# Weight preparation placed beside the first chunk's front, new step tables, and three element-wise steps moved from VectorE to GpSimd in a two-layer recurrent kernel

## What is computed

```python
x = L0_attn_x                                       # (2, 2048, 256)
xn = _layernorm(x)
s = _L0_attn_ref(xn, ...)                           # norm, Mamba block, norm, MLP 256-1024-256
g = _silu(_L0_ffn_ref(xn, w_gate, w_up, w_down))    # FP4-quantized gated MLP, 704 wide
x = x + s * g
xn = _layernorm(x)
s = _L1_attn_ref(xn, ...)                           # 16 heads, attention between the 2 sequences
g = _silu(_L1_ffn_ref(xn, qweights, scales, ...))   # 3 blocks of two 4-bit linears with LoRA
return x + s * g

def _mamba(x, ...):                                 # D_INNER 512, D_STATE 16, 4 taps
    xi, z = jnp.split(x @ in_proj_w, 2, axis=-1)
    xc = _silu(causal_conv(xi, conv_w) + conv_b)
    dt, Bm, Cm = jnp.split(xc @ x_proj_w, [16, 32], axis=-1)
    dt = jax.nn.softplus(dt @ dt_proj_w + dt_proj_b)
    h = exp(dt_t * A) * h + dt_t * B_t * x_t        # for each token t, 512 x 16 states
    y = sum(h * C_t) + D * xc
    return (y * _silu(z)) @ out_proj_w

def fp4_linear(x, w): return fp4(x) @ fp4(w).T      # blocks of 16: amax/6, round to E2M1, scale back
def _qlora_linear(x, q, scale, bias, la, lb):
    return x @ ((q / 7.5 - 1) * scale).T + bias + (x @ la.T) @ lb.T
```

## Time and profile before

| | |
|---|---|
| time, median of 3 runs | 1854.18 us (1853.78 to 1857.8) |
| profiled execution | 1856.52 us, of which the span of the profile is 1854.7 us |
| mean granted clock of PE over the span | 0.953 of full |
| busy share | PE 85%, DVE 84%, ACT 78%, POOL 68% |
| preparation of weights | 0 to 135.6 us |
| front of chunk 0 | 135.6 to 184.5 us |
| steady state | 99.65 us a chunk (861.65 to 961.30) |
| tail | 1757.0 to 1854.7 us |

### The profile page before, as it was taken

How to read it: one execution, slowest core, us unless ns; L and a number is a source line. 1 busy time by engine, 2 the same in 40 slices (tenths; PEclk the granted TensorE clock), 3 DMA queues, 4 the chain that set the end, 5 groups by cost and what they waited for, 6 DMA issues and landing times.

```text
span 1854.7 us, 28175 instructions
## 1 busy us (share of the span) xinstructions
PE 1577.4 (85%) x7632; PEld 1164.4 (63%) x7632; DVE 1551.4 (84%) x2882; ACT 1437.5 (78%) x3076; POOL 1252.4 (68%) x1313
## 2 busy tenths in 40 slices
PE   0083768899999999999989999999989999999875
PEld 0051556586767677776767676767667767767653
DVE  0623999999999999999999999999999999999811
ACT  0034678898989898989889888989888989888723
POOL 0304676777777786868687777778686868787522
PEclk9976789999999999999999999999999999999987
DMA  8000111111111111111111111111111211111100
GB/s 209 0 6 29 52 47 58 47 57 37 58 48 60 43 52 51 59 47 52 52 52 52 44 51 50 58 47 46 58 52 47 63 41 58 46 44 55 35 0 12
DMA packets 68395, 91.70 MB, mean 49 GB/s; under 512 B 15674, under 2 KB 34686, under 8 KB 68238
## 3 DMA queue, kind: packets, MB, share of 16 engines
q1 hardware_dynamic: 68238, 89.91, 15.8%
HBM read 85.17 MB, written 4.72 MB: 48 GB/s over the span
## 4 chain that ended last, share of the span: by engine, by line
PE 27%; POOL 20%; DVE 16%; issue 16%; ACT 12%; POOLq 0%; ACTq 0%; DVEq 0%; DMA 0%
PE bank L511 10%; POOL drive L965 10%; PE bank L627 6%; DVE unit L1127 4%; DVE hc L1133 3%; PE bank L516 2%; PE y_ps L537 2%; ACT unit L742 2%; PE bank L498 1%; PE bank L563 1%; ACT op_a L709 1%; DVE xc L1158 1%; ACT L709 1%; ACT L923 1%; POOL s L1068 1%
## 5 line engine op out<-in xcount | busy, mean ns | idle before, releaser
L965 POOL TENSOR_TENSOR drive<-wx,rows 128x1024 f32<-128x1024 f32 x256 | 604.1, 2360 | 163.3 <-DVE unit L1127 82.8
L1127 DVE TENSOR_TENSOR_SCAN unit<-unit,drive 128x512 f32<-128x512 f32 x512 | 616.7, 1221 | 30.7 <-POOL drive L971 23.4
L742 ACT ACTIVATE unit<-dt,aneg 128x254 f32<-128x254 f32 x1024 | 441.9, 468 | 19.8 <-ACT carry L750 0.7
L1133 DVE TENSOR_TENSOR hc<-unit,rows 128x512 f32<-128x512 f32 x512 | 340.9, 684 | 8.8 <-issue 3.0
L537 PE MATMUL y_ps<-ident,hc 128*128 128x128 f32 x2048 | 278.1, 282 | 52.5 <-DVE hc L1133 52.4
L537 PEld LDWEIGHTS y_ps<-ident,hc 128*128 128x128 f32 x2048 | 241.2, 145 | 115.3 <-DVE hc L1133 71.8
L742 ACT ACT_TABLE_LOAD x109 | 139.8, 1283 | 3.7
L750 ACT ACTIVATE carry<-unit 128x4 f32<-128x4 f32 x512 | 79.3, 169 | 66.8 <-DVE unit L1140 63.0
L627 PE MATMUL bank<-op_a,w_f 128*128 128x256 f32 x512 | 115.7, 385 | 11.2 <-ACT op_a L709 11.2
L709 ACT ACT_TABLE_LOAD x77 | 98.8, 1283 | 22.4 <-PE bank L498 21.6
L511 PE MATMUL bank<-w_f,wide 128*128 128x256 f32 x512 | 113.3, 379 | 1.5 <-ACT wide L709 1.5
(11 more groups left out here) (220 smaller groups left out, 3439.4 us busy)
## 6 DMA issues: line engine op xcount, KB each, us to landing
rows<-rows_scratch SPq DMA_DIRECT2D x256, 256.0 KB, 3.3
x_t<-in_L_attn_x_dram SPq DMA_DIRECT2D x16, 256.0 KB, 3.7
x<-in_L_attn_x_dram SPq DMA_DIRECT2D x16, 256.0 KB, 3.3
out_dram<-x SPq DMA_DIRECT2D x16, 256.0 KB, 2.1
w_f<-in_L_attn_ffn_w_dram SPq DMA_DIRECT2D x2, 1024.0 KB
q_raw<-in_L_ffn_qweights_dram SPq DMA_DIRECT2D x1, 1536.0 KB
w_in<-in_L_attn_in_proj_w_dram SPq DMA_DIRECT2D x1, 1024.0 KB
qkv_raw<-attn_in_proj_weight_dram SPq DMA_DIRECT2D x1, 768.0 KB
```

Source lines behind the costliest of these rows:

```text
L742: last = a_.activation(u[:, k * TOK:(k + 1) * TOK].rearrange("p (b t) -> p b t", b=B)[:, :, 1:TC], dt[p][:, g, :].rearrange("p (b t) -> p ...
L965: g_.tensor_tensor(drive[n % 2][:, :, :].rearrange("p (g b) t -> p g b t", b=B), wx[p][:, :, :].rearrange("p g (b t) -> p g b t", b=B), ro ...
L1127: v.tensor_tensor_scan(u[:, :], u[:, :], d, 0.0, ALU.mult, ALU.add).then_inc(S["scan_done"], 1)
L1133: v.tensor_tensor(hc[n % NPROD][:, 4 * half:4 * half + 4, :].rearrange("p (g b) t -> p g b t", b=B), unit_of(ch, n, half)[:, :].rearrange( ...
```

## The change

Five things are changed. What is computed stays the same.

1. **Preparation beside the first front.** The separate block is gone. x of chunk 0 is loaded first, then the weights in four groups, each with its own semaphore: what the front needs (10 DMAs), the gate weights (3), the 4-bit and LoRA weights (4), the rest. The front steps of chunk 0 (`FRONT`) are written into each engine's stream between the preparation's steps; `due()` leaves them out of the tables afterwards. Raw weights lie in buffers that the scan uses later (`drive`, `hc`, `rows`, `ops`, `hx`, `xs`, `kv`, `hq`, `hq_t`). Turns and folds go through `y_ps` (two buffers) instead of the three banks, and a fold adds the 4-bit matrix by transposes where it used products with the identity.
2. **Waits.** `exp` waits for `dt_ready` only in a chunk's first half-step, `out` and `drive` for `carry_in` only at states 0 and 8, `drive` for `wx_ready` only at state 0, `scan` for its drive and `hc` for `y_summed` only in half a; `hc` waits for its rows no more.
3. **Bias rows.** `bias_row` uses `pick` (a piece of the identity) and `b_two`, both of type float32r and 64 rows high: rows 0 to 5 hold the rounded biases, rows 32 to 37 what the rounding left, all others zero.
4. **Three steps on POOL.** `wx` (dt*xc) is a POOL step; the sum into x (`xadd`) and the sum of context and v (`cadd`) are too. The rest of DVE's `x1` is split into `x1` (gating) and `x1s` (statistics).
5. **New tables** for all five engines. ACT loads its function table 16 times a chunk instead of 19.

```diff
-PE_PLAN, ACT_PLAN, POOL_PLAN, DVE_PLAN, SP_PLAN = ...
+PE_PLAN, ACT_PLAN, POOL_PLAN, DVE_PLAN, SP_PLAN = ...
...
+FRONT = {
+    "SP": ("load", "wr"),
+    "POOL": ("f", "log", "wx"),
+    "ACT": ("xn", "xhf", "u", "tap0", "tap1", "z0", "tap2", "tap3", "z1", "xc0", "xc1", "usave", "xp", "dt0", "dt1",
+            "dtexp", "dtln"),
+    "PE": ("uT", "xi0", "xi1", "z0", "xi2", "xi3", "z1", "xp", "dt0", "dt1"),
+    "DVE": ("f", "conv0", "conv1", "dt"),
+}
...
+def due(engine, name, chunk):
+    return there(chunk) and not (chunk == 0 and name in FRONT[engine])
...
             def bias_row(dst, row, wide_):
-                return t.matmul(dst[:, 0:wide_ * D], ident[0:NROW, row:row + 1].to_broadcast([NROW, P]),
-                                b_rows[:, None, :].to_broadcast([NROW, wide_, D]), start=False, stop=True,
+                return t.matmul(dst[:, 0:wide_ * D], pick[:, row:row + 1].to_broadcast([2 * LOW, P]),
+                                b_two[:, None, :].to_broadcast([2 * LOW, wide_, D]), start=False, stop=True,
                                 skip_group_check=True)
...
+            elif name == "wx":
+                pool.wait_ge(*at("dt_ready", ch))
+                pool.wait_ge(*at("xc_ready", ch))
+                g_.tensor_tensor(wx[p][:, :, :], dt[p][:, :, :], xc[:, :, :], ALU.mult).then_inc(S["wx_ready"], 1)
...
+            elif name == "cadd":
+                pool.wait_ge(*at("attn_dve", ch))
+                pool.wait_ge(*at("v1_copied", ch))
+                g_.tensor_tensor(ctx_[:, :, :], ctx_[:, :, :], v1[:, None, :].to_broadcast([P, B, D]), ALU.add)\
+                    .then_inc(S["ctx_ready"], 1)
+            elif name == "xadd":
+                pool.wait_ge(*at("s_gated", ch))
+                pool.wait_ge(*at("x_again", ch))
+                g_.tensor_tensor(x1[p][:, :, :], x1[p][:, :, :], s0[:, :, :], ALU.add).then_inc(S["x1_ready"], 1)
...
+                pool_step(pool, "f", 0)
+                divide(0)
+                divide(1)
+                unscale(0)
+                divide(2)
+                unscale(1)
+                pool_step(pool, "log", 0)
+                unscale(2)
+                pool_step(pool, "wx", 0)
...
+                dve_step(dve, "f", 0)
+                dve.wait_ge(gate_in, 16 * len(load_gate))
+                scale(0)
+                scale(1)
+                dve_step(dve, "conv0", 0)
+                step_of(0)
+                dve_step(dve, "conv1", 0)
+                round_(0)
+                scale(2)
+                step_of(1)
+                round_(1)
+                dve.wait_ge(lora_in, 16 * len(load_lora))
+                v.tensor_scalar(l_raw, q_raw, 1.0 / 7.5, -1.0, ALU.mult, ALU.add).then_inc(lora_deq, 1)
...
+                step_of(2)
+                round_(2)
+                dve_step(dve, "dt", 0)
```

540 lines of the change are left out of this document (290 added, 250 removed).

## The result

The changed kernel takes 1802.53 us (median of 4 runs, 1800.57 to 1805.73) against 1855.99 for the kernel before in the same comparison; the ratio is 0.9712, 95% interval 0.969 to 0.9735. It is faster by 2.9%, where 1762 us, 5% less, was forecast. The profiled execution has a span of 1801.2 us.

A forecast was written before the change was run, and what follows sets the result against it. GpSimd's queue was taken to bound piece A of each chunk, VectorE's own work piece B, after a start almost without overlap. 1854.7−90.5 (start)+4 (chunks)−6 (last chunk, tail) = 1762 us; own range 1742 to 1782, 8 in 10 1704 to 1786.

The forecast's parts named there:

- First scan at 94: Start: preparation overlapping chunk 0's front brings the first scan to 94 us instead of 184.5, −90.5, bounds −78 and −103.
- 17+37+7+14+8+9: Start, in us: loads 17, VectorE's work 37, hold-up by GpSimd's products 7, folds 14, turns 8, gate to scan0a 9.
- Piece A, +2.6: Chunk boundary, scan11b's end to next scan1a, 33.9 us, set by GpSimd's queue: +2.6 us, bounds 0 to +3.7.
- `dt` between cadd and drive14: Piece A: VectorE's dt add stands between GpSimd's cadd and drive14, +1.2 us, or 0 if it slips beside a gap.
- covered by one microsecond: Piece A: behind cadd, exp14a is done at 17 us and scan14a has its drive at 18, so no cost.
- some 28 us of work: Piece A: behind cadd, TensorE has some 28 us of work or waiting until the last sum, due at 30.
- Piece B, −2.3: Rest of the chunk, scan1a to next scan11b, 65.8 us of VectorE's own work: −2.3 us, bounds −1.5 to −3.5.
- the waits, −1.5: Piece B: VectorE's waits of 0.7, 0.5 and two shorter ones go, −1.5 us a chunk.
- 3.5 us a chunk on TensorE: Bias rows as one instruction instead of two records: 3.5 us a chunk less on TensorE, bounds 0 to 5.
- a rival with chance 0.12: VectorE and GpSimd exclude each other at more cost than counted: chunk 101.3, first scan 100, 1788 us; chance 0.12.
- Rival 3: Slower than before: ctx sum behind log delays ctxT and what follows; needs 6.6 us more a chunk, 106.5; chance 0.02.
- Rival 1: VectorE bounds the chunk and its lighter load counts in full: chunk 95.5 to 97, 1712 us; chance 0.32.

The follow-up runs named there:

- split wait: One semaphore for each of the three gate weights, nothing else, against the changed kernel; 1794.71 us.
- the pair of runs on them: Changed kernel with the five tables of before and three steps back on VectorE, 1773.74 us; the same with float32 two-record bias rows, 1787.32 us.
- the old tables: Changed kernel with the five tables of before and wx, ctx sum and x sum back on VectorE; 1773.74 us.
- the dt*xc kernel: Only dt*xc moved to GpSimd, against the 1762.11 us version with tables of before, turns ahead of folds and split gate-weight waits; 1771.28 us.
- ScalarE's new order: exp13b, exp14b and exp0a moved earlier in ScalarE's table, against the changed kernel with the ctx sum on VectorE (1786.87 us); 1811.78 us.
- the kernel with the earlier down product: TensorE's down product moved right behind sum12, against the kernel with ScalarE's exp13b, exp14b and exp0a moved earlier (1811.78 us); 1783.22 us.

## Why the prediction was wrong

**First scan at 94 (measured 111.45): two terms of the sum.** The steps and their order were right; VectorE's queue of 37+7 us took 44.5. (The terms 17+37+7+14+8+9 add up to 92, not 94.) The step that failed first is the loads: they were put at 17 us, of a stated 10 to 27, and took 28.46: +11.5, and beyond the bound. Of that, 6.9 us pass before the first load is issued, for which the prediction counted nothing, and 4.6 are the loading itself, 21.6 us for 17. The split wait showed that this time goes straight to the end. The folds were put at 14 us, "and 26 at worst", and took 21.7, since the granted clock was 0.50: +7.7. The prediction took the pitch at full clock, though TensorE was to stand idle ahead of them. Turns (8.4 for 8) and the way to the first scan (8.4 for 9) were right. POOL's log and product did hide.

**Piece A, +2.6 (measured +3.2): the queue was right, its cover was not.** The forecast let GpSimd's queue set this piece, +2.6, and drive1's end came 2.5 us later. "POOL never idle between log and drive2 but for the x-rounding" came true (it waited 1.93 us there and nowhere else). Some of its terms were off and made up for each other by luck: `dt` between cadd and drive14 was put at +1.2, but it runs beside drive14 and takes 2.0 to 3.1 us, and it is a fix step of GpSimd beside it that is held, for 0.9; log's start came 0.45 us later, which wasn't forecast. What failed is the step on what waits behind `cadd`: "covered by one microsecond" for exp14a, and for TensorE "some 28 us of work", due at 30. TensorE's last sum ended at 32.1, VectorE waited 5.3 us for ScalarE's decays and not "some 6 us" for drives, and scan1a starts 0.7 us behind drive1's end, where the forecast had nothing. Two things were left out. First, TensorE idle for 5.2 us did not resume at its old pace: the clock is 0.50 behind it, and the 28 us are longer. Secondly, ScalarE's table was not followed: exp13b stands behind dtln with its two table loads, exp14b behind a norm that waits for GpSimd, exp0a behind the gates. What the runs show in its place: 1.2 us of the 3.2 are the ctx sum (0.8 of it GpSimd's queue), 0.3 go with ScalarE's order and the down product's place, and 1.6 are left, at whose end scan1a follows drive1 at once. That these 1.6 are GpSimd's longer queue, 0.4 in log's start and 1.2 behind it, is read from the trace; no run moved it alone.

**Piece B, −2.3 (measured −1.3).** VectorE's work fell by 61.39 − 60.31 = 1.08, as forecast (0.7+0.4). The failed term is the waits, −1.5. Those for TensorE did go with the bias rows, as the pair of runs on them shows, but others took their place in the new tables: 0.8 us for a tap, 0.4 for decays, 0.3 for TensorE, 0.2 for `xadd`, together 1.7 where 1.6 stood before. VectorE's idle time in the piece is 2.9 us, before it was 3.1. This step is the larger part of the chunks' miss: 1.1 us a chunk here, 0.6 in piece A.

**Bias rows.** 3.5 us a chunk on TensorE was right: six records take 2.8 us a chunk, the twelve of before 6.3 together. By the Trainium skill (FP8 and Floating Point Precision, TensorE Precision Notes) true float32 takes four passes. A single pass would bring a 512-column row from 1.2 us to 0.3, an estimate from that count; the trace has 0.49 to 0.50 for 512 columns (0.38 for 256), between the bounds. Their worth was placed wrongly: 0.5 us a chunk in the old tables, not the 1.2 of VectorE's two waits, but 7.2 us in the last chunk and the tail, where 3.5 were forecast.

**The rule on the shared port** was cited against this change and then priced low, as a rival with chance 0.12 in which "POOL's drive0 now ends when DVE's x-rounding is due". This is what the dt*xc kernel shows, 0.53 us turned into 2.51. The prediction cited the rule for two operands; the held step has one, and is a `tensor_scalar`. The Trainium skill names this case too (SBUF — State Buffer, Who interferes with whom): a VectorE step in a mode that uses both ports contends with GpSimd, `tensor_scalar` can enter such a mode, and whoever issues first holds the pair for the whole instruction. The trace agrees with it: such steps take 0.42 to 0.43 us for 512 columns and 0.53 for 704 when nothing holds them, two-operand ones 0.69 and 0.89, and the held one 2.51. The rival's chunk of 101.3 is close to the 101.5 measured, but that is luck: in the changed kernel the x-rounding's first step takes 0.42 us and is not held. Its time, 1788, lies 15 us under the measured 1802.5; it had the first scan at 100, and that is 11 of them.

**Rival 3**, the ctx sum's ring: the sum costs 1.1 us a chunk in all, far from the 6.6 that would have made the kernel slower; the part outside GpSimd's queue, 0.3 of it, the forecast's own sum had at nothing. Rival 1 (chunk at 96.3) is refuted: its mark was that VectorE waits under 4 us a chunk, and it waits 8.8 (7.1 in piece A, 1.7 in B); its lighter load was not paid out in full in the new tables, and not at all in the old ones.

## What to carry to other kernels

Work that is moved from a full engine to an idle one must be priced at three places: what is queued behind it there, which PSUM bank or buffer comes free later for it, and which instructions of the first engine now run beside it. Here three small steps took 2.6 us a chunk off the busiest engine; in one set of tables one of them gained 0.5 us a chunk and another cost 1.1, in the other set the three cost over 50 us together. A preparation that overlaps is as late as its last load: wait for each load where it is used, and look at what the first load itself waits for.

## What the hardware showed

- Behind TensorE's idle time of 5.16 us (changed kernel, ahead of ctxT, all 14 chunks) and of 3.40 us (ScalarE's new order, ahead of the down product, all 13) the granted clock was 0.50 (1.2 GHz), and the next products took longer: 3.57 us for 1.94, 9.31 for 5.93. Behind shorter ones it differed by chunk: 2.02 us with dt*xc and the sum into x on GpSimd in the old tables was followed by the fall in 9 of 13 chunks, 1.98 us in the kernel before in 8 of 12, 2.53 us with the old tables in 4 of 12. In the kernel with the earlier down product the longest wait in piece A is 1.47 us, and the clock stayed at 1.00 (2.4 GHz). The wait of 3.40 us was paid twice: the product behind it took 3.4 us longer.
- The clock fell to 0.50 also in the folds, after five of them at 1.00, with no gap in TensorE's records (a copy every 0.99 us, then every 1.77).
- A one-operand step of VectorE, SBUF to SBUF (a `tensor_scalar` on float32 read as int32), was held for a whole GpSimd product (2.51 us for 0.53). VectorE's scans, which run in PSUM with one operand in SBUF, were not: none of the 512 took over 1.23 us beside the same products.
